# Turning rows at full precision: two products with the raw normalised input in place of four products of rounded parts

## The reference, cut to what matters

```python
def _gn(v, G=32, eps=1e-05):            # per image and group of 6 channels
    m = jnp.mean(g, axis=(1, 2, 4), keepdims=True)
    s = jnp.var(g, axis=(1, 2, 4), keepdims=True)
    return ((g - m) / jnp.sqrt(s + eps)).reshape(v.shape)

def _L2_conv_ref(x, gate_w, fc1_w, ...):
    scores = jax.nn.softmax(xf @ gate_w.T, axis=-1)   # 8 experts
    top_v, top_i = jax.lax.top_k(scores, 2)
    for e in range(8):
        w_e = jnp.sum(jnp.where(top_i == e, top_v, 0.0), axis=-1)
        h = _gelu(xf @ fc1_w[e].T + fc1_b[e])
        out = out + w_e[:, None] * (h @ fc2_w[e].T + fc2_b[e])
    shared = _gelu(xf @ w1_w.T + w1_b) * (xf @ w3_w.T + w3_b) @ w2_w.T + w2_b
    return out + shared

x = x + _L2_conv_ref(_gn(x), ...)
```

## Time and profile before

| | |
|---|---|
| median of three runs | 1853.95 us (1848.35 to 1854.25) |
| the profiled execution | 1853.45 us |
| its span in the profile | 1851.6 us |
| mean granted TensorE clock | 0.789 of 2.4 GHz |
| PE, DVE, ACT, POOL busy | 81%, 69%, 52%, 45% of the span |
| instructions | 51732 |

### The profile page before, as it was taken

The page is one execution under the profiler, slowest core; times in us unless marked ns, Lnnn a source line. Parts: engine busy times, 40 slices in busy tenths (PEclk is TensorE's granted clock), DMA queues, the critical chain, the costliest instruction groups (busy, mean ns, idle before and its releaser), DMA issues. The chain is left out here.

```text
span 1851.6 us, 51732 instructions
## 1 busy us (share of the span) xinstructions
PE 1497.0 (81%) x19315; PEld 1279.7 (69%) x19315; DVE 1284.3 (69%) x4458; ACT 969.5 (52%) x1984; POOL 839.7 (45%) x1067
## 2 busy tenths in 40 slices
PE   4768888888863887889877899899976597888977
PEld 4767777777753776767765667688863586676766
DVE  7877777777767566878866674544435746788874
ACT  3633333333343566888924234555542456788872
POOL 3712222222205055879953111566630415687984
PEclk9955555555576898999975579999985689999998
DMA  3000000000013596667215304223234459666612
GB/s 85 4 3 4 4 4 4 4 4 4 4 54 94 166 248 146 147 158 150 53 46 166 97 19 153 96 86 94 86 87 123 130 148 270 142 154 155 143 27 58
DMA packets 73074, 167.62 MB, mean 91 GB/s; under 512 B 18066, under 2 KB 43290, under 8 KB 70332
## 3 DMA queue, kind: packets, MB, share of 16 engines
q1 hardware_dynamic: 67452, 151.46, 31.2%
q0 software_dynamic: 5376, 12.85, 2.3%
HBM read 96.24 MB, written 67.42 MB: 88 GB/s over the span
## 5 line engine op out<-in xcount | busy, mean ns | idle before, releaser
L993 POOL TENSOR_TENSOR l_arena<-l_arena,l_arena 98x784 fp32r<-98x784 f32 x192 | 354.9, 1862 | 102.8 <-PE l_ps L1102 68.0
L501 PE MATMUL gru_ps_r<-gru_hp,gru_wp 128*128 128x16 f16 x3920 | 199.9, 176 | 67.9 <-DVE gru_hp L476 67.9
L501 PEld LDWEIGHTS gru_ps_r<-gru_hp,gru_wp 128*128 128x128 f16 x3920 | 150.7, 106 | 88.3 <-DVE gru_hp L476 88.3
L1276 DVE TENSOR_REDUCE l_ps<-l_ps 98x4 f32<-98x784 f32 x192 | 187.5, 976 | 8.5 <-PE l_ps L1063 2.9
L501 PE MATMUL gru_ps_n<-gru_hp,gru_wp 128*128 128x16 f16 x3920 | 191.2, 174 | 0.0
L551 POOL TENSOR_TENSOR gru_kept<-gru_keep,l0s_state 128x32 f32<-128x32 f32 x196 | 49.3, 252 | 304.5 <-ACT gru_keep L566 304.5
L1101 PE MATMUL l_ps<-l_arena,l_arena 128*66 128x196 f32 x768 | 161.8, 264 | 24.2 <-POOL l_arena L993 23.3
L564 ACT ACTIVATE gru_reset<-gru_ps_r,gru_unscale 128x32 f32<-128x32 f32 x196 | 56.3, 287 | 216.2 <-PE gru_ps_r L501 216.2
L1216 ACT ACTIVATE l_arena<-l_ps 98x784 fp32r<-98x784 f32 x192 | 158.4, 825 | 4.7
L1219 ACT ACTIVATE l_arena<-l_ps 98x784 f32<-98x784 f32 x192 | 157.0, 818 | 0.0
L1102 PE MATMUL l_ps<-l_arena,l_arena 128*66 128x196 f32 x768 | 155.1, 255 | 0.0
(11 more groups left out here) (370 smaller groups left out, 4572.8 us busy)
## 6 DMA issues: line engine op xcount, KB each, us to landing
l_arena<-qk SPq DMA_DIRECT2D x96, 294.0 KB
qk<-l_arena SPq DMA_DIRECT2D x48, 392.0 KB, 6.1
rel<-l_arena SPq DMA_DIRECT2D x24, 686.0 KB
l_arena<-rel SPq DMA_DIRECT2D x48, 343.0 KB
l_arena<-x SPq DMA_DIRECT2D x32, 294.0 KB, 5.5
qk<-l_arena SPq DMA_DIRECT2D x12, 784.0 KB, 9.0
l_arena<-in_experts_dram SPq DMA_DIRECT2D x8, 1152.0 KB, 7.7
l_arena<-x SPq DMA_DIRECT2D x24, 196.0 KB, 2.8
```

What stands on the lines that cost most here:

```text
L501: last = pe.matmul(out[:, b, B * m:B * m + B], wp[:, wi, g, m, :], hp[:, b, part, B * k:B * k + B], start=False, stop=True, skip_group_che ...
L993: pool.tensor_tensor(pl[:TH, g % 2, :, :], p32[:TH, g % 2, :, :], ph[:TH, g % 4, :, :].bitcast(f32), ALU.subtract).then_inc(pl_ready, 1)
L1276: dve.tensor_reduce(m, ps[:TH, S_BANK:S_BANK + 2, :TB].rearrange("p c (h k) -> p c h k", h=2), AXIS.X, ALU.max).then_inc(mx_ready, 1)
```

## The change

For each half PE now does two products in full float32 precision, straight from `xn`: one 128 deep with the unit matrix and the gate's first 128 rows (`turn_a`), one 64 deep with the gate's last 64 rows and the unit matrix of 64, twice (`turn_b`). Both come ready made from memory. `xn` gets a third slot, and DVE now waits before it writes a slot until both halves that read it are turned, as well as for the low parts. PE waits for `xn_ready` in place of `la_ready` and `lb_ready`. The low parts are still made, since `mixture` reads them. A half has 16 gate sums in place of 24, and `choose` does one addition less. The nine instructions that built the operands are gone.

```diff
-    CHUNK, SLOTS = 4, 4
+    CHUNK, SLOTS, IMAGES = 4, 4, 3
-    xn = arena.place(2 * N, 2, 2, T)
+    xn = arena.place(2 * N, 2, IMAGES, T)
-        ra, rb, rl = s.sb("ra", [128, 128 + 2 * E], f32r), s.sb("rb", [128, E + 128], f32r), s.sb("rl", [64, E + 128], f32r)
+        turn = [s.sb("turn_a", [128, E + 128]), s.sb("turn_b", [64, 128 + E])]
...
-                sp.dma_start(g[:, :, :], ins["gate128"]).then_inc(const_in, 16)
+                for half, name in zip(turn, ("turn_a", "turn_b")):
+                    sp.dma_start(half[:, :], ins[name]).then_inc(const_in, 16)
...
-                pe.wait_ge(gate_ready, 5)
+                pe.wait_ge(const_in, 48)
                 for i in range(HALVES):
                     b = i // 2
                     if i % 2 == 0:
-                        pe.wait_ge(la_ready, b + 1)
-                        pe.wait_ge(lb_ready, b + 1)
+                        pe.wait_ge(xn_ready, 2 * b + 2)
...
-                    pe.matmul(out[:, 0:144], part(b, XA)[:, tok], ra[:, :], start=True, stop=False, skip_group_check=True)
-                    pe.matmul(out[:, 0:136], part(b, LA)[:, tok], ra[:, 0:136], start=False, stop=True, skip_group_check=True)
-                    pe.matmul(out[:, 144:280], part(b, XB)[:, tok], rb[:, :], start=True, stop=False, skip_group_check=True)
-                    pe.matmul(out[:, 144:280], part(b, LB)[:64, tok], rl[:, :], start=False, stop=True, skip_group_check=True).then_inc(turned, 1)
+                    pe.matmul(out[:, 0:E + 128], xn[:, 0, b % IMAGES, tok], turn[0][:, :], start=True, stop=True, skip_group_check=True)
+                    pe.matmul(out[:, E + 128:256 + 2 * E], xn[:64, 1, b % IMAGES, tok], turn[1][:, :],
+                              start=True, stop=True, skip_group_check=True).then_inc(turned, 1)
...
-                dve.tensor_copy(ra[:, 0:128], ident[:, :]).then_inc(const_ready, 1)
...
-                        if b >= 2:
-                            dve.wait_ge(la_ready, b - 1)
-                            dve.wait_ge(lb_ready, b - 1)
+                        if b >= IMAGES:
+                            dve.wait_ge(la_ready, b - IMAGES + 1)
+                            dve.wait_ge(lb_ready, b - IMAGES + 1)
+                            dve.wait_ge(turned, 2 * (b - IMAGES) + 2)
...
-                    link(dve.tensor_tensor(logit, logit, logits[:TH, :, 2 * E:], ALU.add))
```

More of the change, by code:

```diff
@@ L1323, in route @@
 def route(nc, ins, x_dram, arena, rows_dram, logits, ident, packed, w13, w2s, wh, wl, w2h, w2l, moments):
-    CHUNK, SLOTS = 4, 4
+    CHUNK, SLOTS, IMAGES = 4, 4, 3
     XA, XB, LA, LB = range(4)
     x = arena.place(0, 2, N)
-    xn = arena.place(2 * N, 2, 2, T)
-    rows = arena.place(2 * N + 4 * T, SLOTS, 2, 128)
+    xn = arena.place(2 * N, 2, IMAGES, T)
+    rows = arena.place(2 * N + 2 * IMAGES * T, SLOTS, 256)
     with Scope(nc, "ro") as s:
@@ L1346, in route @@
             s.sem(n) for n in "std_ready rstd_ready shift_ready xn_ready xh_ready".split())
-        la_ready, lb_ready, gate_ready, const_ready = (s.sem(n) for n in "la_ready lb_ready gate_ready const_ready".split())
+        la_ready, lb_ready = s.sem("la_ready"), s.sem("lb_ready")
         turned, even_rows, odd_rows = (s.sem(n) for n in "turned even_rows odd_rows".split())
@@ L1357, in part, with gate_sums @@
             return packed(n, a)[:, cols]
+        def gate_sums(i):
+            return ps[:TH, i % 4, 128:128 + 2 * E]
         with nc.Block() as block:
@@ L1377, in _ @@
                         sp.wait_ge(odd_rows, i + 1)
-                    sp.dma_start(rows_dram[i * TH:(i + 1) * TH].rearrange("t (k c) -> t k c", k=2),
-                                 rows[:TH, i % SLOTS, :, :]).then_inc(stored[i % SLOTS], 16)
+                    sp.dma_start(rows_dram[i * TH:(i + 1) * TH], rows[:TH, i % SLOTS, :]).then_inc(stored[i % SLOTS], 16)
                 for slot in range(SLOTS):
                     sp.wait_ge(stored[slot], 16 * HALVES // SLOTS)
+                sp.wait_ge(const_in, 48)
             @block.gpsimd
@@ L1398, in _ @@
                     pool.wait_ge(xn_ready, 2 * b + 1)
-                    pool.tensor_tensor(part(b, LB)[:64], xn[:64, 1, b % 2, :], part(b, XB)[:64].bitcast(f32),
+                    pool.tensor_tensor(part(b, LB)[:64], xn[:64, 1, b % IMAGES, :], part(b, XB)[:64].bitcast(f32),
                                        ALU.subtract).then_inc(lb_ready, 1)
@@ L1459, in _ @@
                             act.wait_ge(stored[i % SLOTS], 16 * (i // SLOTS))
-                        act.activation(logits[:TH, i, :], ps[:TH, i % 4, 128:152], ACT.Copy).then_inc(even_rows, 1)
-                        act.activation(rows[:TH, i % SLOTS, :, :], ps[:TH, i % 4, :304].rearrange("p (k c) -> p k c", k=2)[:, :, :128],
-                                       ACT.Copy).then_inc(even_rows, 1)
+                        act.activation(logits[:TH, i, :], gate_sums(i), ACT.Copy).then_inc(even_rows, 1)
+                        act.activation(rows[:TH, i % SLOTS, :].rearrange("p (k c) -> p k c", k=2), ps[:TH, i % 4, :2 * (128 + 2 * E)].rearrange("p (k c) -> p k c", k=2)[:, :, :128], ACT.Copy).then_inc(even_rows, 1)
             @block.vector
@@ L1476, in _ @@
                 dve.tensor_copy(mean[:, :, :].rearrange("p k b -> p (k b)"), mean_sums).then_inc(mean_copied, 1)
-                dve.wait_ge(const_in, 32)
-                dve.tensor_copy(ra[:, 0:128], ident[:, :]).then_inc(const_ready, 1)
[L1479 to L1487, removed]
                 dve.wait_ge(mean_copied, 2)
@@ L1498, in _ @@
                             dve.wait_ge(x_in[b // CHUNK], 48)
-                        if b >= 2:
-                            dve.wait_ge(la_ready, b - 1)
-                            dve.wait_ge(lb_ready, b - 1)
+                        if b >= IMAGES:
+                            dve.wait_ge(la_ready, b - IMAGES + 1)
+                            dve.wait_ge(lb_ready, b - IMAGES + 1)
+                            dve.wait_ge(turned, 2 * (b - IMAGES) + 2)
                         for k in (1, 0):
-                            dve.tensor_scalar(xn[:, k, b % 2, :], x[:, k, b * T:(b + 1) * T], rstd[:, k, b:b + 1],
+                            dve.tensor_scalar(xn[:, k, b % IMAGES, :], x[:, k, b * T:(b + 1) * T], rstd[:, k, b:b + 1],
                                               shift[:, k, b:b + 1], ALU.mult, ALU.add).then_inc(xn_ready, 1)
@@ L1508, in _ @@
                         dve.wait_ge(xn_ready, 2 * c + 2)
-                        dve.tensor_tensor(part(c, LA), xn[:, 0, c % 2, :], part(c, XA).bitcast(f32), ALU.subtract).then_inc(la_ready, 1)
+                        dve.tensor_tensor(part(c, LA), xn[:, 0, c % IMAGES, :], part(c, XA).bitcast(f32), ALU.subtract).then_inc(la_ready, 1)
                     if b >= 3:
@@ L1512, in _ @@
                         dve.wait_ge(turned, i + 1)
-                        dve.tensor_copy(logits[:TH, i, :], ps[:TH, i % 4, 128:152]).then_inc(odd_rows, 1)
+                        dve.tensor_copy(logits[:TH, i, :], gate_sums(i)).then_inc(odd_rows, 1)
                         if i >= SLOTS:
                             dve.wait_ge(stored[i % SLOTS], 16 * (i // SLOTS))
-                        dve.tensor_copy(rows[:TH, i % SLOTS, :, :],
-                                        ps[:TH, i % 4, :304].rearrange("p (k c) -> p k c", k=2)[:, :, :128]).then_inc(odd_rows, 1)
+                        dve.tensor_copy(rows[:TH, i % SLOTS, :].rearrange("p (k c) -> p k c", k=2), ps[:TH, i % 4, :2 * (128 + 2 * E)].rearrange("p (k c) -> p k c", k=2)[:, :, :128]).then_inc(odd_rows, 1)
 def product_packed(pe, out, wh, wl, packed):
@@ L2145, in experts_layer @@
         arena = Arena(nc, s, "l2_arena", ARENA)
-        logits, ident = s.sb("logits", [128, HALVES, 3 * E]), s.sb("ident", [128, 128])
+        logits, ident = s.sb("logits", [128, HALVES, 2 * E]), s.sb("ident", [128, 128])
         w13, w2s = arena.place(AT_TILES + 4 * TB, 2, 2, F), arena.place(AT_TILES + 12 * TB, FB, C)
@@ L2235, in lay_out_experts @@
     o["avg_out128"], o["avg_back"] = (np.ascontiguousarray(x.astype(np.float32)) for x in (out128, back))
-    o["gate128"] = np.ascontiguousarray(twice(a["L2_conv_gate_w"]).transpose(2, 1, 0))
+    gate = a["L2_conv_gate_w"].T
+    o["turn_a"] = np.ascontiguousarray(np.concatenate([np.eye(128), gate[:128]], 1).astype(np.float32))
+    o["turn_b"] = np.ascontiguousarray(np.concatenate([gate[128:], np.eye(C - 128), np.eye(C - 128)], 1).astype(np.float32))
     o["first"] = np.ascontiguousarray(np.broadcast_to(np.arange(E, 0, -1, dtype=np.float32), (TH, E)))
```

1 line of the change is left out of this document (removed).

## The result

The changed kernel took 1859.33 us (median of 7 runs, 1851.51 to 1863.1); the kernel before, in the same series, 1847.94 us (7 runs). Ratio **1.0052, 95% interval 1.0033 to 1.007**: slower by about half a percent, as forecast (1861). The ratio is an estimate from all runs of the series and not the quotient of the two medians, which is 1.0062. Two later series, both on one chip, gave 1.0039 (1.0022 to 1.0055) and 1.0037 (1.0014 to 1.0060). The forecast of +7.5 us is a ratio of 1.0040. A ratio always stands to runs of before in the same series; from series to series the median of before goes from 1848 to 1868 us.

What follows compares the result with a forecast made beforehand. PE was taken to set the route's pace. The stage's end +7.9 us and choose -0.46 summed to +7.5 us on the profiled 1853.45: forecast 1861 us, own range 1858 to 1865, wider range 1848 to 1867.

Steps and rivals of the forecast that it cites:

- The new half: PE's products for one half in the route: 1.402 us against 1.053, with weight loads exposed only where depth changes.
- The bound without handovers: Lower bound for a half in the route if changes of depth cost nothing: four streams of 0.227, 0.908 us.
- The 24 halves: Route from the ninth half on: 24 x 1.402 = 33.6 us, last ending at 1036.1, +7.9 us at the stage's end.
- The start: Start of the route: PE no longer waits for low parts and begins near 990.3, saving 1.3 us at first.
- The ninth half: In the route, it waits for a bank behind the first store; added constants delay it 0.35 us, to 1002.5.
- The mixture's start: Start of the block's next part: later by the route's +7.9 us, the tail between them unchanged.
- choose: Ranking in the mixture: one addition less on DVE's chain, all of it coming out of PE's wait, -0.46 us.
- DVE: its time an image: DVE's work in the route: 1.66 us an image against 2.80 for PE, so its new wait costs nothing.
- rival 1: Clock rises to 2.4 GHz in the route, also if an unbroken stream lifts it: 1847 us; chance 0.10.
- Rival 2: In the route, changes of depth cost nothing and the clock stays: a half 0.908 us, total 1849 us; chance 0.04.
- third rival: In the route, every weight load is exposed: a half 1.896 us, total 1876 us; chance 0.07.
- Rival 4: Shared expert meets another clock: 5.7 us less gives 1855 us, chance 0.19; the reverse, up to 7 us more, 1868.

Runs made afterwards that it cites:

- e1: Changed kernel with the two products of every odd half in swapped order, so an image has two changes of depth, not four; ratio to before 1.0010.
- e2: Changed kernel with turn_b padded by 64 rows of zeros, so the route's second product is 128 deep too; ratio to before 0.9978.
- again: The changed kernel as it is, run and profiled a second time in a later series; 1875.1 us, ratio to before 1.0039.
- third: The changed kernel as it is, run and profiled a third time in another later series; 1868.6 us, ratio to before 1.0037.
- e7: Kernel before with turn_a and turn_b loaded ahead of x but read by nobody; ratio to before 1.0007.
- e4: Changed kernel with the loads of turn_a, turn_b and the unit matrix issued behind the first four images' x; ratio to before 1.0061.
- e3: Kernel before with the fourth product of a half made 128 deep by zeros in rl below row 64; ratio to before 0.9991.
- e5: Changed kernel with every 64 deep product in the route and in the shared expert made 128 deep; ratio to before 0.9901.
- e8: Changed kernel with the unit matrix copied on POOL from turn_a in place of a 64 KB load; ratio to before 1.0041.
- e6: Kernel before with every 64 deep product in the route and in the shared expert made 128 deep; ratio to before 0.9906.

## Why the prediction was right, and which terms were off

- *The new half: right.* 1.402 us forecast, 1.40 measured. e1 (1.15 a half) and e2 (0.91) show its two parts, loads exposed only where the depth changes and four streams of 0.227. The bound without handovers, 0.908, was that of e2. Full precision alone doesn't explain it: it would have left 1.40 in e1 and e2. One of its sources was weaker than it looks: the prediction took 0.21 us between the two instructions of the earlier trace rows from their ends, which are modelled, and their starts are 0.17 apart. It is e2 that measures the 0.227.
- *The 24 halves: right.* Forecast, from the ninth half to the mixture: +7.55 (24 x 1.402 = 33.6 against 26.05). Measured: 1039.37 - 1002.26 = 37.11 against 29.58, so +7.53.
- *The start: seen in two of three.* A gain of 1.3 us was forecast; again and third show 1.1 and 1.0, the first profile none, because there DVE waited for x. It made no difference, as the ninth half takes it back.
- *The ninth half: the mis-sized term.* I took +0.35 us from bytes over the rate of the queue. It was +2.11, +0.77 and +1.37 in the three profiles, and PE did wait for the bank, 1.4 us. e7 shows +1.54 from the loads alone. Bytes over GB/s was too little; how the loads delay the store behind them I can't say, and e4 shows only that moving them doesn't help.
- *The mixture's start* was hence +9.64, +8.29 and +8.89 against the one profile of before, where +7.9 was forecast.
- *choose: the chain is shorter as forecast, its start was overlooked.* From DVE's first addition to PE's product with the choice it takes 6.06 to 6.07 us in all nine profiles with the change, and 6.52 to 6.53 in all four without it: the 0.46. But the prediction counted from the mixture's start, and DVE first waits for the load of mx_first: the chain starts 2.9 to 3.8 us into the mixture, at another time in each profile. In the first profile of the changed kernel it was late, at 3.84 us against 3.29 for L1966 before, and PE waited 0.95 us; in the other two it waited 0.21 and 0.40, where 0.4 was forecast. The late one:
```profile
1043.21 0.42 DVE L1955 TENSOR_TENSOR l_logits<-l_logits 98x256 f32<-98x256 f32 x1 [6.77 <-DMA mx_first<-in_first_dram]
```
- *DVE: its time an image was read too low.* The 1.66 us came from 21.62 us for "about 13 images". In that window DVE made 20 of the two L1503 of an image, so ten images, and three of the 20 lasted 1.4 to 2.4 us. It did no harm in the changed kernel, where PE sets the pace. But it is one reason why rival 1's 19.9 us for twelve images and the 20 to 21 expected of e3 were too short: from the ninth half to the end of the last, e2 took 23.8 and e3 23.6.
- *Rival 1 (clock rises): not for this kernel.* It stayed at 0.50 in all three profiles. But its last clause came true in e2: the unbroken stream did lift it, to a ratio of 0.9978, where 1847 us is one of 0.9963.
- *Rival 2 and 3: fell* by the pace of 1.40. The third was the rule of the Trainium skill (TensorE: Matmul & The Clock Gate, Part 3, The mechanism), that a load overlaps only where the row groups differ. e2 and e5 measure the opposite: all products on the same 128 rows and every load hidden. The prediction's reading of the rule doesn't give its third rival: with the two loads at equal depth exposed and the two handovers hidden, a half also sums to 2 x 0.474 + 2 x 0.227 = 1.402. So the changed kernel's pace doesn't decide against that reading. e1 does, where fewer handovers made the image shorter, and e2, where none did. The same section also lets a load overlap that goes to a background weight buffer, which the prediction left out; no run here can tell whether that is what hides the loads.
- *Rival 4 (another clock in the shared expert): real, but not decisive.* With equal work the stretch to the expert took 158.7, 158.5, 157.9 and 154.7 us, at a mean granted clock of 0.81 to 0.83, and 151.0 in e7 and 152.0 in e8, at 0.87 and 0.85. The spread, 7.9 us with e3's 158.9, is about the size that I gave it. The ratios of the three series stayed within 1.0037 to 1.0052.

The size was right partly by luck. Two errors cancel: the ninth half cost 0.4 to 1.8 us more than forecast, and the stretch to the expert gave back 0.2 to 4. In the first pair of profiles the 1.99 us from the layers ahead of the block come on top. And the 1859 us are near the forecast 1861 also because the median of before fell from 1853.95 to 1847.94 with four more runs: as a difference, 7.5 us were forecast, the first ratio gives 9.6, and the other two about 7.

## What to carry to other kernels

Count changes of depth before counting products: at 1.2 GHz each cost the weight load plus 0.08 us here, 0.25 in the route's full precision products, and zero rows that make a 64 deep product 128 deep cost PE nothing (0.227 us an instruction in e2). Two products at full precision in place of four reduced ones are no gain, and no loss, once the depths are equal (e5 against e6). Before speeding PE up, look at the next engine, and look at its longest instructions and not at its mean: of the some 25 us taken from PE's busy time in the shared expert, 11 came out of the stretch. And compare busy times only at equal granted clock.

## What the runs showed of the hardware that I had not expected

- With all products 128 deep at full precision and no gaps, PE was given 2.4 GHz in the route (e2, from 1010.9 us, after 6.15 of 6.20 us busy), while the changed kernel with PE equally "busy" (33.64 of 33.70 us) stayed at 1.2: the busy share of the profile, which here holds exposed loads, doesn't tell whether the clock will rise.
- Some 100 KB of small constants at the head of a queue moved the ninth half, which waits for a store some 10 us behind them, by 0.8 to 2.1 us, against 0.35 by their bytes.
- The same DVE instruction took 0.38 us as a rule and up to 2.41 while POOL worked on the weights (e2, e3).
